# A gated scan layer and an eight-expert layer, software-pipelined on one core: experts picked by sorting, terms moved to GpSimd, fewer and larger transfers, new orders

## The reference, cut to what matters

```
h = layernorm(x) * (1 + ca) + sa
h = rmsnorm(h);  v = h @ W_v.T;  gates = softmax(h @ W_a.T)      # (8, 512, 8 heads, 16, 17)
new[i] = sum_j gates[i, 1+j] * state[j] + gates[i, 0] * v[i]     # one step per token, 512 in a row
x = x + ga * (h + ys @ W_out.T)
h = layernorm(x) * (1 + cb) + sb
logits = h @ router.T + bias                                     # 8 experts
combine = softmax over the 4 largest logits, 0 elsewhere
act = (clip(up) + 1) * min(gate, 7) * sigmoid(1.702 * gate)      # each expert: 128 -> 2 x 256
x = x + gb * sum_e combine_e * (act_e @ down_e.T + down_bias_e)
```

## Time and profile before

| | |
|---|---|
| three runs | 788.27, 792.42, 794.17 us; median 792.42 |
| profiled execution | 789.0 us, span 787.3, mean granted clock 0.917 |
| busy | DVE 678.0 us (86%), PE 589.9, POOL 567.5, ACT 552.2 |
| transfers | 85.34 MB, queue q1 busy 46.3% of 16 engines |

### The profile page before, as it was taken

The page is one execution under the profiler, slowest core; times in us unless marked ns, Lnnn a source line. Parts: engine busy times, 40 slices in busy tenths (PEclk is TensorE's granted clock), DMA queues, the critical chain, the costliest instruction groups (busy, mean ns, idle before and its releaser), DMA issues.

```text
span 787.3 us, 12543 instructions
## 1 busy us (share of the span) xinstructions
PE 589.9 (75%) x2826; PEld 441.0 (56%) x2826; DVE 678.0 (86%) x2921; ACT 552.2 (70%) x1272; POOL 567.5 (72%) x635
## 2 busy tenths in 40 slices
PE   5785144787968697877878686979788785878986
PEld 3242022565746475665657474757666574757875
DVE  4569999999999999999999999999989999888331
ACT  4764142777786878787777878786867776657885
POOL 2685556687878797888878787978878686735554
PEclk9886565899999999999999999998989997889998
DMA  6265645453726455364537273644545463720000
GB/s 189 83 145 139 139 116 137 102 130 83 171 79 149 107 122 120 79 159 81 129 95 160 77 159 97 134 115 116 117 79 122 108 141 86 163 71 8 14 8 7
DMA packets 162234, 85.34 MB, mean 108 GB/s; under 512 B 77752, under 2 KB 156784, under 8 KB 157936
## 3 DMA queue, kind: packets, MB, share of 16 engines
q1 hardware_dynamic: 162160, 84.55, 46.3%
HBM read 44.66 MB, written 39.85 MB: 107 GB/s over the span
## 4 chain that ended last, share of the span: by engine, by line
DVE 66%; PE 14%; issue 10%; ACT 5%; POOL 3%; DMA 1%; SPq 1%; POOLq 0%; ACTq 0%; DVEq 0%
DVE ps L854 15%; DVE prod L846 14%; DVE ps L860 8%; DVE act_t L926 7%; DVE nmax L824 6%; DVE zs L831 6%; PE ps L1184 6%; PE ps L1197 4%; DVE rz L837 3%; PE ps L1171 2%; ACT ex L590 1%; ACT ps L624 1%; POOL ex L414 1%; ACT up L618 1%; DMA gates<-gate_dram 1%
## 5 line engine op out<-in xcount | busy, mean ns | idle before, releaser
L1184 PE MATMUL ps<-h2t,wgu 128*128 128x256 f32 x1024 | 256.4, 393 | 24.6 <-ACT up L618 24.6
L1184 PEld LDWEIGHTS ps<-h2t,wgu 128*128 128x128 f32 x1024 | 192.6, 196 | 71.4 <-ACT up L618 29.8
L1171 PE MATMUL ps<-wl,ht 128*128 128x512 f32 (+1 forms) x320 | 168.4, 629 | 71.5 <-ACT lg L601 67.6
L1197 PE MATMUL ps<-wd,act_t 128*128 128x128 f32 x1024 | 146.5, 288 | 65.7 <-DVE act_t L926 65.6
L1197 PEld LDWEIGHTS ps<-wd,act_t 128*128 128x128 f32 x1024 | 135.3, 200 | 95.4 <-DVE act_t L926 84.9
L854 DVE TENSOR_REDUCE ps<-prod 128x8 f32<-128x136 f32 x512 | 152.5, 298 | 10.6
L846 DVE TENSOR_TENSOR prod<-gates,ps 128x136 f32<-128x136 f32 x512 | 147.1, 287 | 14.7 <-DMA gates<-gate_dram 6.4
L421 POOL TENSOR_TENSOR lg<-lg,nmax 128x1088 f32<-128x1088 f32 x64 | 130.3, 2039 | 15.0 <-DVE nmax L824 13.1
L676 ACT ACTIVATE weighted<-ps,comb 128x128 f32<-128x128 f32 x256 | 79.9, 363 | 85.4 <-PE ps L1197 83.1
L461 POOL TENSOR_SCALAR up<-up 128x512 f32<-128x512 f32 x128 | 78.4, 612 | 79.3 <-ACT up L618 75.2
L414 POOL TENSOR_TENSOR ex<-ex,rz 128x1088 f32<-128x1088 f32 x64 | 129.2, 2039 | 8.8 <-DVE rz L837 5.7
(11 more groups left out here) (122 smaller groups left out, 586.0 us busy)
## 6 DMA issues: line engine op xcount, KB each, us to landing
gate_dram<-ex SPq DMA_DIRECT2D x256, 136.0 KB, 3.3
gates<-gate_dram SPq DMA_DIRECT2D x32, 1088.0 KB, 5.5
yt_tok<-y_dram SPq DMA_DIRECT2D x256, 8.0 KB, 3.4
xg<-in_L_attn_x_dram SPq DMA_DIRECT2D x32, 64.0 KB
y_dram<-ys SPq DMA_DIRECT2D x32, 64.0 KB, 2.0
out_dram<-res_out SPq DMA_DIRECT2D x32, 64.0 KB
wa_rows<-in_L_attn_W_a_dram SPq DMA_DIRECT2D x1, 1088.0 KB, 5.7
dn_rows<-in_L_ffn_down_proj_dram SPq DMA_DIRECT2D x1, 1024.0 KB, 12.3
```

Of the source, the lines that this page charges most:

```text
L1171: nc.tensor.matmul(ps[:, n % 2, 0:w], ht[:, g % RH, j * P:(j + 1) * P], wl[:, k * LC:k * LC + w], start=True, stop=True).then_inc(lg_ps.se ...
L1184: last = nc.tensor.matmul(gu_ps(m, k, which)[:, q * N:(q + 1) * N], wgu[:, k, rows + q * P:rows + (q + 1) * P], h2t[:, m % 2, :], start=Tr ...
L1197: last = nc.tensor.matmul(dn_ps(j), act_t[:, k % 2, q * N + j * P:q * N + (j + 1) * P], wd[:, k, q, :], start=(q == 0), stop=(q == KI - 1))
```

## The change

Router: `nc.vector.max` sorts the 8 logits; places 5 to 8 of the sorted list are overwritten with 2^127, and `match_replace` puts -2^127 in each place of the logits that equals one of the first four. All router tiles are in SBUF now. `mean_term` moves to GpSimd as two instructions, right behind `inv_sqrt`. The products are written over the gates, 128 elements a row, and the sums read all 17. Gate stores and scan-result loads take two batches each: 4 transfers per tile. `up`, `act_t` and `weighted` have three buffers for two. The orders of all four compute engines change.

```diff
-                for b in range(B):                       # store_gates; load_y likewise
-                    sp.dma_start(gate_dram[j, b // 2, :, b % 2].rearrange("r t e -> t r e"), ex[b * TS:(b + 1) * TS, ...
+                for q in range(B // 2):
+                    sp.dma_start(gate_dram[j, q].rearrange("r b t e -> (b t) r e"), ex[2 * TS * q:2 * TS * (q + 1), ...
+            def mean_term(mv, rs, rs_ok, nm, nx_ok, nm_ok, c):        # GpSimd
+                nc.gpsimd.tensor_tensor(nm[:, :, 0], mv[:, :, 0], rs[:, :, 0], ALU.mult).then_inc(nx_ok.sem, 1)
+                pool.wait_ge(nx_ok.sem, nx_ok.at(c, 1))
+                nc.gpsimd.tensor_scalar(nm[:, :, 0], nm[:, :, 0], -1.0, 0.0, ALU.mult, ALU.add).then_inc(nm_ok.sem, 1)
     GpSimd run:
     inv_sqrt 1
+    mean_term 1
     clamp_up 0
+    clamp_up 1
     finish
-    first_h
     gate_value 0
-    clamp_up 1
     norm_gates 0,0  norm_gates 0,1
     accumulate 0
+    first_h
     clamp_up 2
     gate_value 1  norm_gates 1,0  norm_gates 1,1
+    accumulate 1
     clamp_up 3
     new_residual
-    accumulate 1
     accumulate 2
+    clamp_up 4
     sub_max 0,0
     inv_sqrt 2
+    mean_term 2
-    clamp_up 4
     clamp_up 5
-    accumulate 3
     second_h
+    accumulate 3
     accumulate 4
     clamp_up 6
+    accumulate 5
     sub_max 0,1
-    accumulate 5
     clamp_up 7
-    sub_max 1,0
     accumulate 6
     inv_sqrt (rms)
+    sub_max 1,0
     sub_max 1,1
     ScalarE run, its beginning:
-    weigh_expert 7 / exp 0 / logits_out 0 / exp 1 / up_and_silu 0 / up_and_silu 1 / normalise / logits_out 1, 2, 3
-    combine_out / weigh_expert 0 / logits_out 4 / bias_out / up_and_silu 2
+    exp 0 / weigh_expert 7 / up_and_silu 0 / logits_out 0 / up_and_silu 1 / exp 1 / logits_out 1, 2, 3 / normalise
+    combine_out / bias_out / weigh_expert 0 / logits_out 4 / up_and_silu 2
     TensorE run, its beginning:
-    logits 0 / gate_up 0 / logits 1 / gate_up 1 / logits 2 / turn_combine / logits 3, 4 / down 0 / down_bias / gate_up 2
+    logits 0 / gate_up 0, 1 / logits 1, 2, 3 / turn_combine / down 0 / logits 4 / down_bias / gate_up 2
     VectorE:
-                    prod[:, :].rearrange("p (i k) -> p i k", k=M1),
-                    gates[:, t, :].rearrange("p (i k) -> p i k", k=M1),
+                own = gates[:, t, :].rearrange("p (i k) -> p i k", k=M1)[:, :, 1:M1]
+                nc.vector.tensor_tensor(own, own, state[:, (t - 1) % TS, :].unsqueeze(1).broadcast_to([P, HALF, M]),
+                                        ALU.mult).then_inc(scan.sem, 1)
             def router_ranks(p, n):
+                n == 1: for j in range(TILES): nc.vector.max(top[:, j, :], rl[:, j, :])
+                n == 2: nc.vector.tensor_tensor(rdl[:, :, :], rl[:, :, :], top[:, :, 0:1].broadcast_to([P, TILES, E]), ALU.subtract)
+                        nc.vector.memset(top[:, :, TOP_K:E], BIG)
+                n == 3: for j in range(TILES): nc.vector.match_replace(out=left[:, j, :], in_to_replace=top[:, j, :], in_values=rl[:, j, :], imm_value=-BIG)
             def combine_weights(m, n):
+                n == 0: nc.vector.scalar_tensor_tensor(out=rsl[:, :, :], in0=left[:, :, :], scalar=-BIG, in1=rex[:, :, :], op0=ALU.is_equal, op1=ALU.mult)
+                n == 1: tensor_reduce rsum; n == 2: reciprocal rrec
+                n == 3: nc.vector.tensor_tensor(comb[:, m % 2, :, :], rsl[:, :, :], rrec[:, :].unsqueeze(2).broadcast_to([P, TILES, E]), ALU.mult)
```

More of the change, by code:

```diff
@@ L159, in adaln_block @@
         rl = sb("rl", [P, TILES, E])
-        rmx = sb("rmx", [P, TILES])
-        rgt = sb("rgt", [P, TILES, E, E])
+        top = sb("top", [P, TILES, E])
+        left = sb("left", [P, TILES, E])
+        rsl = sb("rsl", [P, TILES, E])
         rdl = sb("rdl", [P, TILES, E])
@@ L493, in run @@
                     accumulate(m, 0)
+                if a is not None:
+                    first_h(a)
+                if m is not None:
                     clamp_up(m, 2)
@@ L884, in router_ranks @@
+                    for j in range(TILES):
+                        nc.vector.max(top[:, j, :], rl[:, j, :]).then_inc(rank_in.sem, 1)
                 elif n == 2:
-                    dve.wait_ge(rank_in.sem, rank_in.at(p, 4))
-                    nc.vector.tensor_tensor(rdl[:, :, :], rl_ps, rmx[:, :].unsqueeze(2).broadcast_to([P, TILES, E]),
+                    dve.wait_ge(rank_in.sem, rank_in.at(p, 3))
+                    nc.vector.tensor_tensor(rdl[:, :, :], rl[:, :, :], top[:, :, 0:1].broadcast_to([P, TILES, E]),
@@ L887, in router_ranks @@
                                             ALU.subtract).then_inc(rank_in.sem, 1)
-                    nc.vector.tensor_tensor(req, req, lower[:, :, :].unsqueeze(1).broadcast_to([P, TILES, E, E]), ALU.mult
-                                            ).then_inc(rank_in.sem, 1)
-                elif n == 3:
-                    nc.vector.tensor_tensor(rgt[:, :, :, :], other, own, ALU.is_gt).then_inc(rank_in.sem, 1)
-                else:
-                    dve.wait_ge(rank_in.sem, rank_in.at(p, 7))
-                    nc.vector.tensor_tensor(rgt[:, :, :, :], rgt[:, :, :, :], req, ALU.add).then_inc(rank_in.sem, 1)
+                    nc.vector.memset(top[:, :, TOP_K:E], BIG).then_inc(rank_in.sem, 1)
+                else:
+                    dve.wait_ge(rank_in.sem, rank_in.at(p, 5))
+                    for j in range(TILES):
+                        nc.vector.match_replace(out=left[:, j, :], in_to_replace=top[:, j, :], in_values=rl[:, j, :],
+                                                imm_value=-BIG).then_inc(rank_in.sem, 1)
@@ L1285, in run @@
                     gate_up(m, 3)
-                if g is not None:
-                    logits(g, 6)
                 if p is not None:
```

348 lines of the change are left out of this document (152 added, 196 removed).

## The result

| | before | after |
|---|---|---|
| runs | 792.96 us median (788.27 to 794.17, 4 runs) | 843.59 us median (841.50 to 844.82, 4 runs) |
| span of the profiled execution, mean clock | 787.3 us, 0.917 | 842.9 us, 0.839 |
| first and last product | 58.12, 727.97 | 56.18, 783.21 |
| mean of the eleven full iterations | 43.21 us | 47.65 us |

The ratio is 1.0635, 95% interval 1.059 to 1.068: slower, as forecast, but by 51 us where 14 were forecast, and outside the range.

What follows compares the result with a forecast made beforehand. VectorE was taken to bound the kernel. To 789.0 us it added +20.4 for eleven full iterations, +2.2 for the other five, -3.6 ahead of the scan and -2.4 for waits already counted: 806 us, range 776 to 824.

Steps and rivals of the forecast that it cites:

- eleven full iterations: Scan iterations priced at +1.9 us each, from VectorE's work, holds, late chain and Exp: +20.4 in all.
- the other five: Remaining scan iterations: -3.9 us for VectorE's work, +6.1 for holds and the late chain in two, so +2.2.
- ahead of the scan: Before the first product: norm_gates earlier by 2.6 us and fewer store transfers saving 1, together -3.6 us.
- behind the last product: Tail of TensorE's gate_up and down in turn, order unchanged: 0 us (-2 to +1).
- The -2.4: Waits of gated_out for TensorE at the lower clock, about 2.4 us in two full iterations, taken off as already counted.
- VectorE's work: Shorter products, cheaper router and both mean_term gone from VectorE: -1.1 us an iteration.
- the holds: rdl, rsl and comb, with two SBUF inputs, stand still beside GpSimd's instructions: +2.2 us an iteration (0 to 6.1).
- second Exp: On ScalarE between two up_and_silu, with four table loads for two, making row_sum 1,0 late: +0.2 us an iteration (0 to 1.3).
- late chain ahead of `hidden` 3: comb in slot 27, then TensorE, ScalarE and GpSimd work before hidden 3: +0.6 us an iteration (0 to 1.6).
- The reading of the hold: With two inputs in SBUF, VectorE stands still until GpSimd's running instruction has ended.
- The rival that had the Exp later than forecast: Two table loads with 1.4 us drain each make Exp 2.8 us later an iteration: 836 us, chance 0.04.
- Parts at nothing: mean_term on GpSimd, the third buffer, the other gate stores and scan loads, and the tail: no cost or gain.

Runs made afterwards that it cites:

- e6: The changed kernel with the slots and orders of the kernel before, and rl, left and rsl in PSUM: 773.23 us, ratio 0.981.
- e5: The changed kernel, its orders kept, with rl, left and rsl in PSUM, so no VectorE loop instruction has two SBUF inputs: 800.70 us, ratio 1.015.
- e4: The changed kernel with surplus, unread TensorE matmuls ahead of logits 3, turn_combine and down 7: 815.07 us, ratio 1.033.
- e7: e5 with surplus matmuls before logits 3, turn_combine and down 7, only in iterations with a router stage: 777.83 us, ratio 0.986.
- e9: e5 with ScalarE's second Exp ahead of both up_and_silu, as in the kernel before: 782.80 us, ratio 0.985.
- e15: e6 with ScalarE's second Exp moved behind up_and_silu 0 and 1: 797.36 us, ratio 1.007.
- e1: The changed kernel, all its parts kept, with the slots and engine orders of the kernel before: 790.94 us, ratio 1.0005.
- e2: The changed kernel with only rsl moved to PSUM, orders as changed: 802.84 us, ratio 1.017.
- e8: The kernel before, with its own router and transfers, in the run orders and slots of the changed kernel: 813.50 us, ratio 1.031.
- e11: e5 with its new VectorE slots, but TensorE, ScalarE and GpSimd in the orders of the kernel before: 847.03 us, ratio 1.066.

## Why the prediction was wrong

By its own sum, between the two profiled executions (789.0 and 844.8 us), in us:

| term | predicted | measured |
|---|---|---|
| eleven full iterations | +20.4 - 2.4 | +48.8 (4.44 each) |
| the other five | +2.2 | +8.4 |
| ahead of the scan | -3.6 | -1.9 |
| behind the last product | 0 | +0.4 |

Eleven times its own +1.9 would be 20.9; the slip of 0.5 us changes nothing. The -2.4 came as forecast: the waits of `gated_out` for TensorE fell from 2.4 us in the eleven iterations to 0.3. A full iteration splits again, and the runs give each part a number:

| part of a full iteration | predicted | measured, undone in this order |
|---|---|---|
| VectorE's work | -1.1 | -1.2 (before to e6) |
| the late chain and the Exp, by the orders | +0.8 | +2.3 (e6 to e5) |
| the holds | +2.2 | +3.3 (e5 to after) |

- **VectorE's work, -1.1 an iteration: right.** e6 shows 1.1 less running time once nothing stands in its way.
- **The failed step: VectorE's waits, put at +0.8 an iteration (second Exp +0.2, late chain ahead of `hidden` 3 +0.6), and measured at +3.65.** VectorE waited 3.95 us in a full iteration of the kernel after, 0.30 in one before; its running time rose by 0.67 only, where the forecast had +1.1 with the holds. What it waited for in the eleven full iterations (us in total, times, longest):

```profile
DVE act_t L904 <- ACT ps L625: 22.1, 22, 1.5
DVE zs L822 <- ACT ex L593: 17.7, 10, 1.8
DVE act_t L904 <- POOL up L465: 2.3, 8, 0.4
```

The wait for the Exp is 1.6 us an iteration, above the upper end that I gave it (1.3). The first line is `hidden` 2 with 1.5 and `hidden` 4 with 0.5, for which the sum has nothing. The chain that I did charge, `clamp_up` to `hidden` 3, is 0.2 here and 0.7 in e5, as sized. I had followed `logits_out` 1 on to TensorE and had written down the 4.5 us of idle time (measured 4.21), but charged the lower clock behind it only to the chain from `comb` to `hidden` 3. At the lower clock everything of TensorE was late: `gate_up` 2 and Silu 2 and so `hidden` 2, the bias, `accumulate` 0. The idle stretch ahead of `down` 7 slowed `logits` 0 and delayed `gate_up` 0, `up_and_silu` 0 (by 1.71 us), and so the Exp itself, which I had let start on time.
- **That this runs through the clock is shown by e4 and e7**, where surplus matmuls hold it at 1.00: the waits fall to 0.1 and 0.3 us an iteration with the Exp in its new place. The Exp's place is worth 18 us in e5 against e9 (1.2 an iteration) and 24 in e6 against e15 (2.0). That each late instruction leads to the next idle stretch, a loop, I read from the order of events in the traces; no run opens it at one link only.
- **The reading of the hold was too wide.** I had written that VectorE stands still until GpSimd's running instruction has ended. In the traces of all kernels that is so beside `sub_max` and `norm_gates` (85 of 85 instructions with both inputs in SBUF that began inside one) and beside `clamp_up` (24 of 26; the other two began in its last 0.07 us). Beside the power of `inv_sqrt`, 0.70 us on 2 elements with its inputs in SBUF, it is never so: 48 began inside one, and none took over 0.19 us. One of them in the kernel after:

```profile
416.41 0.70 POOL L404 TENSOR_TENSOR rms<-me,minus_half 128x2 f32<-128x2 f32 x1
416.57 0.17 DVE L871 TENSOR_TENSOR rdl<-rl,top 128x16 f32<-128x16 f32 x1
```

Whether the number of elements or the operation decides it, no run tells.
- **Which instructions stand still: right for `comb`.** 1.2 was worked out, and it stood 1.3 (1.44 less its usual 0.17). `rsl` was put beside `inv_sqrt`, where it fell, at 0.15, and by the last point it costs nothing there; beside `sub_max` 1,1, in e1, it stood 1.2. `rdl`, put at 1.4, stood 1.7 in e2 and e4 and not at all in the kernel after: it began at 416.57, 0.5 us ahead of `sub_max` 1,0 (417.07). GpSimd had waited 0.68, 0.36 and 0.63 us for ScalarE in the 16 us before, in e2 once 0.30; I take these for the cause. So the 2.2 of the forecast was held in neither kernel: 2.9 in e4, 1.3 in the kernel after. The holds end within 0.04 us of GpSimd's instruction, and moving one input to PSUM, with nothing else changed, took each away (e2, e5, e6).
- **The holds' price.** `comb` stood 1.3 us, and without it (e2) an iteration is 2.9 shorter, 41 us in all. TensorE's `turn_combine` waits 1.35 us for it in a full iteration of the kernel after and 0.05 in e2; the clock there is 0.83 and 0.91, and the wait of `hidden` 2 for Silu 1.5 and 0.03. With the clock kept at 1.00 in both, e4 against e7, two holds of 2.9 us in sum are worth 2.6 an iteration, about their own length. That e4's 45.07 meets the forecast's 44.9 is in part luck: the holds are worth 2.6 there for 2.2, and the orders 0.5 (e6 to e7) for 0.8, which had been worked out for the lower clock.
- **These shares don't add.** Undone singly in the changed kernel, the Exp gives 25 us, the tiles' place 43, the clock 28, together more than the 51 lost: they overlap in the same waits.
- **Ahead of the scan.** The transfers saved the 1 us that I took: stores and landing took 9.07 us (43.11 to 52.18), now 8.07, as the issue is shorter (3.50 for 6.26) and the landing longer (4.6 from the issue for 3.3):

```profile
42.01 3.50 SPq L324 DMA_DIRECT2D gate_dram<-ex  x4
50.08 0.34 SPq L331 DMA_DIRECT2D gates<-gate_dram  x1
```

`norm_gates` began at 37.88 for 38.98, 1.1 earlier and not 2.6. Part of this can't be told apart: e1 and e6 have the same order there and their first products lie at 57.95 and 55.45.
- **The table loads** are as the forecast counted, four in a full iteration for two before, at 1283 ns. The rival that had the Exp later than forecast was right in its effect and wrong in its cause: the Exp was 1.7 us late by the wait for TensorE. A drain is not seen: the Exp at 379.63 starts 0.01 us behind the end of the load that began at 378.34. The Trainium skill, ScalarE: Activation LUTs, "What ACT_TABLE_LOAD costs", puts 1.38 us of drain beside the load; this trace doesn't show it.

```profile
L593 ACT ACT_TABLE_LOAD x13 | 16.7, 1283 | 0.2
```

- **Parts at nothing.** `mean_term` on GpSimd and the transfers are free: e6 contains them and runs at its VectorE sum. So is the third buffer, and it shows no gain either: e8 runs the new orders with two.

**Still open**: which of the five scan iterations outside the full ones carries how much, and why the matmuls behind one and the same idle stretch of 2.74 us are slow in some iterations of e6 and fast in others. The runs show that filling three stretches brought the mean clock from 0.839 to 0.959 (after to e4) and from 0.896 to 0.948 (e5 to e7).

## What to carry to other kernels

An order written by hand is tuned as one: the slots of one engine without the orders of the others (e11) cost as much as all of it together, with no hold in them. When an instruction is moved, follow each thing that stands behind it to the engine with a variable clock, and price an idle stretch there by the work that it slows afterwards, not by its own length. And keep one input of a small VectorE instruction in PSUM where GpSimd runs long ones: it was a change of three tile addresses, worth 2% in the old orders (e1 to e6) and 5% in the new (after to e5).

## What the hardware showed

- A VectorE instruction with two SBUF inputs of 16 elements took 1.49, 1.47 and 1.90 us for 0.17, and ended with the GpSimd `tensor_tensor` of 2.04 us that ran beside it. With one of them in PSUM it took 0.17, in the same slot. Beside GpSimd's power of 0.70 us on 2 elements it took 0.17 with both in SBUF too.
- Surplus work made a kernel faster: about 18 unread matmuls an iteration took 23 us off e5.
- Eight-element router instructions: `max` 155 ns, match load 81, `match_replace` 150, memset 65; two `max` in a row took 0.23 us.
